# Two-head sums on GpSimd, fused normalising and moved projections in a transformer block on one Trainium2 core

## The reference

```python
def _tc_rmsnorm(x, t, gw, gb, bw, bb):
    g = (t @ gw.T + gb)[:, None, :]
    b = (t @ bw.T + bb)[:, None, :]
    inv_rms = jax.lax.rsqrt(jnp.mean(x * x, axis=-1, keepdims=True) + EPS)
    return g * x * inv_rms + b

def _attention(x, Wq, Wk, Wv, Wo):          # 16 heads of 32
    q, k, v = (x @ Wq.T, x @ Wk.T, x @ Wv.T)  # reshaped to (B, L, H, dh)
    attn = jnp.einsum('blhd,bmhd->bhlm', q, k) / scale
    p = jax.nn.softmax(attn, axis=-1)
    o = jnp.einsum('bhlm,bmhd->blhd', p, v).reshape(B, L, D)
    return o @ Wo.T

def _swiglu(x, gate_w, hid_w, out_w):
    return jax.nn.silu(x @ gate_w.T) * (x @ hid_w.T) @ out_w.T

x1 = x + _attention(_tc_rmsnorm(x, t, g1w, g1b, b1w, b1b), Wq, Wk, Wv, Wo)
x = x + x1 + _swiglu(_tc_rmsnorm(x1, t, g2w, g2b, b2w, b2b), gate_w, hid_w, out_w)
```

## Time and profile before

| | |
|---|---|
| median of 3 runs | 2371.1 us (2369.59 to 2376.34) |
| the profiled execution | 2371.89 us, of which the span in the trace 2370.0 us |
| TensorE busy | 2247.4 us (95%) |
| VectorE busy | 1647.2 us (70%) |
| GpSimd busy | 1419.5 us (60%) |
| ScalarE busy | 1283.8 us (54%) |
| attention | from the start to about 1375 us of the span |

### The profile page before, as it was taken

How to read it: one execution, slowest core, us unless ns; L and a number is a source line. 1 busy time by engine, 2 the same in 40 slices (tenths; PEclk the granted TensorE clock), 3 DMA queues, 4 the chain that set the end, 5 groups by cost and what they waited for, 6 DMA issues and landing times.

```text
span 2370.0 us, 38915 instructions
## 1 busy us (share of the span) xinstructions
PE 2247.4 (95%) x10848; PEld 1565.9 (66%) x10848; DVE 1647.2 (70%) x2723; ACT 1283.8 (54%) x2286; POOL 1419.5 (60%) x1331
## 2 busy tenths in 40 slices
PE   5999989999989999899999889999999999999999
PEld 4655447555457554466554468887888788888887
DVE  4777745777736777546777378877887788778877
ACT  3367772567763667735666644363436344544454
POOL 0299981699952899915999846504660367036712
...
GB/s 192 149 96 64 83 34 99 88 77 65 59 103 51 97 56 90 32 112 66 64 54 32 111 138 54 39 153 210 54 36 134 222 65 36 111 201 109 43 88 179
DMA packets 96454, 221.94 MB, mean 94 GB/s; under 512 B 15712, under 2 KB 15712, under 8 KB 94560
## 3 DMA queue, kind: packets, MB, share of 16 engines
...
q10 hardware_dynamic: 432, 6.29, 0.7%
...
...
## 4 chain that ended last, share of the span: by engine, by line
PE 75%; DVE 8%; issue 7%; ACT 4%; POOL 2%; SPq 2%; DMA 2%; DVEq 0%; ACTq 0%; POOLq 0%
PE bank L1869 26%; PE bank L1883 12%; PE bank L976 9%; PE bank L1100 8%; PE bank L1055 7%; PE bank L1161 6%; DVE pmax L800 3%; PE bank L1086 3%; PE bank L1065 2%; POOL sums L539 2%; SPq L381 2%; ACT qk_hi L617 1%; PE bank L1041 1%; DVE ow L1689 1%; DMA wo_raw<-in_out_w 1%
## 5 line engine op out<-in xcount | busy, mean ns | idle before, releaser
L800 DVE TENSOR_REDUCE pmax<-bank 128x1 f32<-128x512 f32 x1024 | 645.4, 683 | 177.5 <-PE bank L1055 171.5
L539 POOL TENSOR_TENSOR sums<-sums,probs_up 128x512 f32<-128x512 f32 x432 | 540.3, 1285 | 0.1
L1055 PE MATMUL bank<-ks,qs 96*128 96x512 f32 x1024 | 421.2, 422 | 36.2 <-DVE pmax L800 34.6
L1161 PE MATMUL bank<-qs,ks 128*128 128x512 f32 x1024 | 421.2, 416 | 15.0 <-ACT probs L701 8.3
L1883 PE MATMUL bank<-ow,aw 128*128 128x512 f32 x1536 | 360.6, 392 | 2.8 <-DVE ow L1689 2.7
L1869 PE MATMUL bank<-H_hi,wt_hi 128*128 128x512 f32 x896 | 350.5, 391 | 8.5 <-DVE H_lo L1724 8.3
L1869 PE MATMUL bank<-H_lo,wt_hi 128*128 128x512 f32 x896 | 349.8, 390 | 0.0
L1869 PE MATMUL bank<-H_hi,wt_lo 128*128 128x512 f32 x896 | 349.6, 390 | 0.0
L701 ACT ACTIVATE probs_up<-bank 128x512 f32<-128x512 f32 x512 | 283.3, 607 | 97.5 <-PE bank L1161 91.2
L701 ACT ACTIVATE probs<-bank 128x512 f32<-128x512 f32 x512 | 286.9, 602 | 86.3 <-PE bank L1161 78.7
L1883 PEld LDWEIGHTS bank<-ow,aw 128*128 128x128 f32 x1536 | 285.0, 188 | 65.3 <-issue 7.1
...
## 6 DMA issues: line engine op xcount, KB each, us to landing
...
wo_raw<-in_out_w SPq DMA_DIRECT2D x128, 256.0 KB, 2.8
qs<-qk_hi SPq DMA_DIRECT2D x256, 64.0 KB, 2.0
ks<-qk_hi SPq DMA_DIRECT2D x128, 128.0 KB, 2.4
...
qs<-qk_lo SPq DMA_DIRECT2D x128, 64.0 KB, 2.0
...
```

Of the source, the lines that this page charges most:

```text
L539: nc.gpsimd.tensor_tensor(total, first, probs(s, h), ALU.add) \
L800: nc.vector.reduce_max(pmax[:, t, h, hf:hf + 1], mbank[n % MB][:], AX_X).then_inc(sq_done, 1)
L1055: nc.tensor.matmul(mbank[n % MB][:], qs[0:96, u % 3, h, t * P:(t + 1) * P], ks[0:96, u // 2 % 2, h, hf * QB:(hf + 1) * QB], start=True, st ...
L1161: nc.tensor.matmul(sbank[i % SB][:], ks[:, g % 2, h, s * P:(s + 1) * P], qs[:, u % 3, h, :], start=True, stop=True).then_inc(st_ready, 1)
```

## The change

The diff, cut to what carries the text:

```diff
-Q_EVEN = {2: 12, 4: 9}
-PROJECTED = {("K", 2, 1): (0, 1), ("Q", 2): (12, 1)}
+PROJECTED = {("K", 2, 1): (0, 1), ("Q", 2): (12, 1), ("Q", NU - 1): (5 * UNIT - 2, 2), ("Q", NU): (6 * UNIT + 8, 1),
+             ("K", NU, 0): (7 * UNIT + 8, 1), ("K", NU, 1): (7 * UNIT + 13, 1)}
 for odd in (1, 3):
-    PROJECTED.update({("Q", odd + 2): (odd * UNIT, 1), ("K", odd + 3, 0): (odd * UNIT + 14, 1),
-                      ("K", odd + 3, 1): ((odd + 1) * UNIT, 1), ("Q", odd + 3): ((odd + 1) * UNIT + Q_EVEN[odd + 1], 1)})
+    PROJECTED.update({("Q", odd + 2): (odd * UNIT - 2, 2), ("K", odd + 3, 0): (odd * UNIT + 8, 1),
+                      ("K", odd + 3, 1): ((odd + 1) * UNIT - 2, 2), ("Q", odd + 3): ((odd + 1) * UNIT + 8, 1)})
-HT_AT = {(4, 15): (0, 0), (5, 8): (1, 0), (5, 12): (2, 0), (5, 16): (3, 0),
+HT_AT = {(4, 23): (0, 0), (5, 8): (1, 0), (5, 16): (2, 0), (5, 23): (3, 0),
          (7, 0): (0, 1), (7, 1): (1, 1), (7, 4): (2, 1), (7, 6): (3, 1)}
-MAXIMA_AT = (6, 3)
+MAXIMA_AT = (7, 0)
+NORMALISE_AT = {(1, 2): 0, (1, 3): 1, (2, 0): 2, (2, 1): 3}
-def act_reads(tile):
-    return (tile[0], tile[-1]) != ("D", 1)
+def act_reads(tile, body=True):
+    return (tile[0], tile[-1]) != ("D", 1) and not (body and in_maxima_bank(tile))
+HEADS = 2
+SUMS = QUADS * (QT - 1) * GH // HEADS
+    def sum_places(u, quad, heads):
+        if u < NU - 1 and quad == 0 and heads == 0:
+            return o[:, NG - 1, :].rearrange("p (h c) -> p h c", h=HEADS)
+        return sums[:, HEADS * heads:HEADS * heads + HEADS, :]
 # GpSimd
-                    if s == 4 and 0 < u < NU - 1:
-                        normalise(b, u - 1)
-                    for h in range(GH if s % QT else 0):
-                        pool.wait_ge(st_done, SCORES_T(b, NT + n * GH + h + 1) + SB)
+                    for heads in range(GH // HEADS if s % QT else 0):
+                        pool.wait_ge(st_done, SCORES_T(b, NT + n * GH + HEADS * heads + HEADS) + SB)
+                        if s % QT == 1 and (heads == 1 or u == NU - 1):
                             pool.wait_ge(w_ready, MISC(b, sums_before(b, u, s // QT)))
+                        total = sum_places(u, s // QT, heads)
+                        first = probs_of(s - 1, heads) if s % QT == 1 else total
+                        nc.gpsimd.tensor_tensor(total, first, probs_of(s, heads), ALU.add) \
                             .then_inc(sum_done, 1)
 # ScalarE
-                        if (s, h) == (1, 1) and u:
-                            output(b, u - 1)
-                        if u == NU - 1 and (s, h) == (2, 3):
-                            denominators_up(b)
 # VectorE
+                if body and in_maxima_bank(tile):
+                    link(nc.vector.tensor_scalar(bank[:], bank[:], cur_gain[:, k:k + 1], cur_bias[:, k:k + 1], ALU.mult, ALU.add))
+                    link(nc.vector.tensor_copy(hT[0][:, k, cols], bank[:]))
-                dve.wait_ge(od_act, b * NU + (u + 2))
+                dve.wait_ge(pv_done, b * (NU * PAIRS) + (u + 1) * PAIRS + 2)
-                nc.vector.tensor_tensor(cols, cols, den[:] if u == NU - 1 else mspare[:], ALU.mult).then_inc(on_done, 1)
+                nc.vector.tensor_tensor(cols, obank[:], den[:], ALU.mult).then_inc(on_done, 1)
-                        if s == 3 and 0 < u < NU - 1 and h < 3:
-                            normalise(b, u - 1, h)
+                        if u and (s, h) in NORMALISE_AT:
+                            normalise(b, u - 1, NORMALISE_AT[s, h])
 # TensorE
             if pair == 0:
-                pe.wait_ge(od_act, b * NU + (u + 1))
+                pe.wait_ge(on_done, b * NU + (u + 1))
+            out_tile(b, len(EARLY_OUT), slice(None))
             values(b, NU - 1, PAIRS - 1)
             denominators(b, NU - 1, QUADS - 1)
-            for t in range(len(EARLY_OUT), NT - 2 if last else NT):
+            for t in range(len(EARLY_OUT) + 1, NT - 2 if last else NT):
```

More of the change, by code:

```diff
@@ L142, in done_at, with in_maxima_bank @@
     return [m for m in (made_at(u, s, h), tile if part == KT - 1 else None, sums_at(u, s, h)) if in_batch(b, m)]
-def act_reads(tile):
-    return (tile[0], tile[-1]) != ("D", 1)
+def in_maxima_bank(tile):
+    return tile[0] == "hT" and tile[2] == 1
+def act_reads(tile, body=True):
+    return (tile[0], tile[-1]) != ("D", 1) and not (body and in_maxima_bank(tile))
 def dve_reads(tile):
@@ L156 @@
 MISC = Counter(len(LEAD_MISC), len(BODY_MISC))
-MISC_ACT = Counter(sum(map(act_reads, LEAD_MISC)), sum(map(act_reads, BODY_MISC)))
+MISC_ACT = Counter(sum(act_reads(m, False) for m in LEAD_MISC), sum(map(act_reads, BODY_MISC)))
 LEAD_DVE = [m for m in LEAD_MISC if dve_reads(m)]
@@ L201, in sums_done @@
 def sums_done(b, u, s, h):
-    return b * (NU * SUMS) + (SUMS * (u + 1) + GH * (s // QT * (QT - 1) + max(s % QT, 1) - 1) + h + 1)
+    return b * (NU * SUMS) + (SUMS * (u + 1) + GH // HEADS * (s // QT * (QT - 1) + max(s % QT, 1) - 1) + h // HEADS + 1)
 def act_before(b, tile):
     order = order_of(b)
-    return sum(map(act_reads, order[:order.index(tile)]))
-def in_maxima_bank(tile):
-    return tile[0] == "hT" and tile[2] == 1
+    return sum(act_reads(m, b is not None) for m in order[:order.index(tile)])
 def wbank_before(b, tile):
@@ L596, in work_tile @@
                 n = hf * KT + k + 1
-                act.wait_ge(full, n if b is None else b * (NHALF * KT) + (NHALF * KT + n))
+                act.wait_ge(full, n if b is None else b * KT + (NHALF * KT + n))
                 nc.scalar.activation(hT[0][:, k, cols], bank[:], ACT.Copy).then_inc(w_act, 1)
@@ L696, in batch @@
                         act.wait_ge(st_ready, SCORES_T(b, i + 1))
-                        if s % QT != 1:
+                        if s % QT != 1 and h % HEADS == 0:
                             act.wait_ge(sum_done, sums_done(b, u, s - QT, h) if s >= QT
@@ L711, in batch @@
                         for tile in done_at(u, s, h, b):
-                            if tile[0] != "D":
+                            if tile[0] != "D" and act_reads(tile):
                                 work_tile(b, tile)
@@ L728, in batch @@
                             act.dma_start(wv[:].bitcast(F32), wv_dram).then_inc(wv_loaded, 16)
-            output(b, NU - 1)
             output_hi(b, len(SPLIT_AT))
@@ L779, in work_tile @@
             dve.wait_ge(w_ready, MISC(b, misc_index(b, tile) + 1))
-            if act_reads(tile):
+            if act_reads(tile, body):
                 dve.wait_ge(w_act, MISC_ACT(b, act_before(b, tile) + 1))
@@ L829, in normalise @@
                 link(nc.vector.reciprocal(pair[:, 1, :], cols[:, :, 0]))
-            elif part == 2 and u == NU - 1:
+            elif part == 2:
                 link(nc.vector.transpose(den[:], pair[:, 1, :].unsqueeze(2).to_broadcast([P, QB // 32, 32])))
-            elif part == 2:
-                nc.vector.transpose(den[:], pair[:, 1, :].unsqueeze(2).to_broadcast([P, QB // 32, 32])).then_inc(den_ready, 1)
-            else:
-                dve.wait_ge(od_act, b * NU + (u + 2))
-                if u < NU - 1:
-                    dve.wait_ge(den_up, b + 1)
+            else:
+                dve.wait_ge(pv_done, b * (NU * PAIRS) + (u + 1) * PAIRS + 2)
                 cols = o[:, u // 2, u % 2 * QB:(u % 2 + 1) * QB]
-                nc.vector.tensor_tensor(cols, cols, den[:] if u == NU - 1 else mspare[:], ALU.mult).then_inc(on_done, 1)
+                nc.vector.tensor_tensor(cols, obank[:], den[:], ALU.mult).then_inc(on_done, 1)
         def weight_hi(w, half=0):
@@ L988, in evicted @@
         def evicted(b, tile):
-            pe.wait_ge(w_act, MISC_ACT(b, act_before(b, tile) + 1))
+            if act_reads(tile, b is not None):
+                pe.wait_ge(w_act, MISC_ACT(b, act_before(b, tile) + 1))
             pe.wait_ge(w_dve, MISC_DVE(b, dve_before(b, tile) + 1))
@@ L1064, in denominators @@
             for h in range(GH):
-                last = nc.tensor.matmul(wbank[DH * h:DH * h + DH, :], ones[:], sum_place(quad, h), start=True,
+                last = nc.tensor.matmul(wbank[DH * h:DH * h + DH, :], ones[:], sum_places(u, quad, h // HEADS)[:, h % HEADS, :], start=True,
                                         stop=not direct)
@@ L1199, in attention_program @@
         "exps": [(st_done, SCORES_T(b, NT + NU * NS * GH) + SB)],
[L1200 removed]
+        "affine": [(full, NHALF * KT + (NB - 1) * KT), (w_dve, MISC_DVE(b, 0))],
         "norm": [(x_scaled, NB * 8), (inv_ready, NB * 2)],
         "stacks": [(s, NB * NU * HEAD_INC) for s in q_stacked] + [(s, NB * NG * HEAD_INC) for s in k_stacked],
[L1203 removed]
+        "values": [(pv_done, NB * NU * PAIRS + 2), (on_done, NB * NU + 1), (sum_done, sums_done(b, NU - 1, NS - 1, GH - 1))],
         "denominators": [(w_dve, MISC_DVE(b, dve_before(b, ("D", NU - 1, 1)) + 1))],
```

49 lines of the change are left out of this document (9 added, 40 removed).

## The result

The changed kernel takes 2397.2 us (median of 4 runs, 2395.5 to 2402.2), the kernel before beside it 2370.4 us (2368.0 to 2376.3): a ratio of 1.0106, 95% interval 1.0091 to 1.0121. It is slower by some 26 us, where I forecast no change, and outside my range of 2349 to 2388. The profiled execution of the changed kernel is the slowest of the four (2402.2 us), so its trace holds some 5 us more than the median.

The account below looks back on a forecast made before the run. Within a unit TensorE was taken to wait for VectorE; GpSimd was full but rarely waited for. Terms of +0.55 us per batch three times (+1.6) and -1.3 in the last made +0.3 on 2371.9: forecast 2372, range 2349 to 2388.

Parts of the forecast that it names:

- 6th: four normalising pieces and a token tile in six steps without a projection to cover them, +0.8, step 23 again +2.1: 6th unit, first three batches: these two charges, less 1.0 us of waiting for the sums, made +1.9 us.
- 8th unit's head: Start of the 8th unit: TensorE's low granted clock there would recover, counted as 0.7 us gained per batch.
- 6th and 7th of the last batch: Last batch's 6th and 7th units: bound by the sums before, then by VectorE at 30.1 us, -2.1 us.
- the slot's wait: Middle units: second projection waits for copies out of its slot; +1.1 us in the 3rd, -0.15 in 2nd and 4th.
- mT, -0.5 us in each of seven units: Maxima's transpose one step later: its 0.5 us wait goes behind step 28's scores, gaining that in seven units.
- Normalising, nothing by itself: ScalarE's eviction and GpSimd's product were off the path, so moving that work to VectorE gains nothing by itself.
- Pairs: Two-head sums on GpSimd: 2379 ns by straight line, about 2.35 us start to start; no gain in the first five units.
- The rival with two singles: Slower rival: a two-head sum on GpSimd costs 2.57 us, kernel at 2384 us; chance 0.14.
- Seventh to eighth unit: Chain from D to D shortens from 33.1 to 30.7 us, -2.4, plus 0.7 per batch gained from the clock.
- Output tile first: Batch end: output tile fills the last exponential's wait but delays D; +1.35 us per batch, +1.7 in the last.
- VectorE falls behind at the moved token tiles: Slower rival: step 23 tiles hold mT past the next step 0; 5th and 6th lose 2 us more each, 2384; chance 0.14.
- First and fifth unit: First unit: only mT, -0.5 us. Fifth, first three batches: waits at steps 27 and 28 behind the token tile, +1.6.

Follow-up runs that it names:

- cover6: Changed kernel with the 7th query tile's projection moved to steps 8 to 11 of the 6th unit and the first token tiles at other steps: 2377.6 us.
- mT_alone: Kernel before with only the maxima's transpose one step later (step 28 for 27): 2385.6 us, ratio 1.0055.
- tokens_alone: Kernel before with only the four token tiles of the last unit put on VectorE alone: 2369.1 us, ratio 0.9983.
- norm_only: Kernel before with two-head sums, fused normalising at steps 6 to 9 and VectorE's last-unit token tiles: 2406.6 us, ratio 1.0138.
- three_back: Changed kernel with first token tiles, projections' steps and the third output tile's place taken back together: 2418.1 us, ratio 1.0189.
- proj_before: Changed kernel with the projections back at their old steps: 2431.3 us, ratio 1.0245.
- tail_before: Changed kernel with the third output tile back behind the last denominators: 2390.8 us, ratio 1.0075.
- mT_back: Changed kernel with the maxima's transpose back at step 27: 2391.6 us, ratio 1.0087.

## Why the prediction was wrong, point by point

**The step that failed: "6th: four normalising pieces and a token tile in six steps without a projection to cover them, +0.8, step 23 again +2.1".** The places were right: TensorE waits at steps 10 to 12 and at 26 to 28. What the sum left out is the granted clock that falls behind such a wait. In batch 1, steps 9 to 13 take 9.6 us against 6.2 and steps 26 to 30 take 10.2 against 5.5: 8.0 us, of which two slow sixteens are 4.4. Batch 2 runs the same instructions at a mean clock of 0.95 instead of 0.84 and loses 3.8 us instead of 7.9: 4 us come with the clock. An estimate from the same rows: the missing clock is worth at most 0.05 x 37.4 = 1.9 us in batch 2, which leaves some 2 us for the waits, about my +1.9. Summed at +1.9, the unit lost 6.6 us on average in the first three batches, 14 us over my sum. I counted the clock as a gain at the 8th unit's head and never as a price of the waits that I had found myself. `cover6` agrees: the same work elsewhere, the normalising beside a projection, no fall of the clock in this unit, 19.6 us less.

Unit by unit, my sum missed the two traces by 30 us: 14 in this unit, 14 in the 1st to 4th units of all four batches (mT and the part at step 30, less the slot's wait, all below), and 4.6 in the 6th and 7th of the last batch, which I had at -2.1 and which came out at +2.5, with slow values in both. The 5th units took 4 us less than I had summed; the rest nearly cancels.

**mT, -0.5 us in each of seven units.** Wrong in sign: +0.35 (`mT_alone`). I took the wait before mT for time that mT costs; it was a wait of VectorE's queue which the next matmul has to sit out anyway. Over 28 units that is 24 us against my sum, in size the largest mis-sized term, in part paid back by the next point.

**The slot's wait, +1.1 us in the 3rd and 5th.** The wait is there: ScalarE stands for the `qs` and `ks` copies 17 times in the changed kernel (one of them ahead of the first batch), 2.26 us in the third unit; I had said 1.5 to 3 us, some 16 times. But the slot is free 177.40 - 169.57 = 7.8 us behind step 6, not 8.9: K's copies took 9.5 us here and not the 10.4 of the fifth unit before, where an issue lasted longer, and my sum had 0.2 us more than its rows give (1.6 + 10.4 - 3.3 = 8.7). From step 6 to step 21's maximum the third unit takes 182.96 - 169.57 = 13.4 us: -0.1 and not +1.1. The 3rd unit comes out at +0.3, mT's 0.35 in it.

**Normalising, nothing by itself.** True in the middle units of the changed kernel, by the cover that I named for GpSimd and ScalarE but not for VectorE: the second projection. I priced the two edits as independent; each without the other costs 34 to 41 us.

**Pairs.** Right: 2385 ns against 2379, and GpSimd 28.3 us in the third unit. The Trainium skill, page "GPSIMD Engine Reference", section 3.1, has 4497 ns for 2048 columns, and the estimate of 2356 ns from it lies 1.2% below the rows. The rival with two singles (2570 ns) is out.

**Seventh to eighth unit.** -3.1 with the clock; measured -4.4, -2.8 and -3.4. `tokens_alone` shows the 8th unit's part. The 7th unit's 1.6 us are in neither part alone (-0.2 for the pairs). In the traces they come in steps: -0.6 with the fused normalising besides (`norm_only`), -1.2 with the later mT too (`three_back`), -1.6 with the token tiles' new steps (`proj_before`).

**Output tile first.** +1.35 us a batch, measured 0.9, 2.6, 2.7, and 0.9 at the end for my 1.7; `tail_before` gives back 6.3 us by its median. The mechanism is right; in batches 2 and 3 the price is too low by the clock behind the wait.

**VectorE falls behind at the moved token tiles.** This rival had mT, late behind the tiles at step 23, hold up the next unit's step 0. That wait is not there: step 31 of the 5th and 6th unit takes 0.46 to 0.47 us in every batch. The 6th unit did cost more than I summed, but in steps 10 to 13 and 26 to 29 and by the clock; the 5th cost less.

**First and fifth unit.** The first has +1.1 for my -0.5: 0.7 us is a projection's part that now stands at step 30, the rest mT (batch 2: `proj_before` has 34.9 us for 35.6, `mT_back` 35.3). Each later unit gives such a part to the one before and takes one from the next; the 6th only gives, so its waits and clock cost 0.7 us more than its length shows. My sum had neither. The fifth was charged +1.6 and came out at +0.9, -0.5 and +0.8.
